# Thirty-eight expert tiles placed inside the routing steps of an attention and expert kernel, b3 folded into centred weights, the table of tiles made in four parts

## The reference, cut to what matters

```python
x = x + conv(ln_c(x))        # q, k, v by 128 x 64 weights; k, v softmaxed over an image
t = to_tokens(x)
logits = einsum('bsd,de->bse', ln_t(t), Wg)
top_logits, top_idx = top_k(logits, 2);  top_w = softmax(top_logits)
h = einsum('bsd,edf->bsef', ln_t(t), W1)
g = einsum('bsd,edf->bsef', ln_t(t), W3) + b3
t = t + einsum('bse,bsef,efd->bsd', C, silu(h) * g, W2)     # C: top_w at the two chosen experts
```

## Time and profile before

| what | value |
|---|---|
| runs, median (lowest to highest) | 329.83 us (326.42 to 330.59) |
| profiled execution, span | 344.2 us |
| mean granted TensorE clock | 0.787 |
| TensorE busy | 255.7 us, 74% |
| VectorE busy | 233.2 us, 68% |
| ScalarE busy | 184.4 us, 54% |
| GpSimd busy | 182.1 us, 53% |
| moved by DMA | 29.78 MB |

### The profile page before, as it was taken

One profiled execution on the slowest core, in us unless ns is written; L12 is line 12 of the kernel. 1 busy time (PEld: TensorE's weight loads), 2 busy tenths in 40 slices (PEclk: granted clock), 3 DMA queues, 4 the chain that ended last, 5 costly groups with the idle time before them and its releaser, 6 DMA issues.

```text
span 344.2 us, 7292 instructions
## 1 busy us (share of the span) xinstructions
PE 255.7 (74%) x1560; PEld 220.5 (64%) x1561; DVE 233.2 (68%) x835; ACT 184.4 (54%) x471; POOL 182.1 (53%) x233
## 2 busy tenths in 40 slices
PE   4786949474848574340999999999999999999300
PEld 1444636453636463110999999999999899999200
DVE  3658676675655565640688878887888788878823
ACT  2636638273635332310577777776777677777200
POOL 4094274452717273770066656665666557666800
PEclk9986855565555555585799999999999999999855
DMA  4879210110101010131133222221222212136068
GB/s 112 286 229 352 77 55 23 39 35 29 47 16 43 22 54 23 55 101 32 41 85 82 71 59 59 72 62 47 61 61 61 61 54 70 46 93 214 33 203 292
DMA packets 31904, 29.78 MB, mean 87 GB/s; under 512 B 5202, under 2 KB 29588, under 8 KB 31748
## 3 DMA queue, kind: packets, MB, share of 16 engines
q1 hardware_dynamic: 24208, 18.11, 18.2%
q0 software_dynamic: 4320, 8.92, 7.7%
q10 hardware_dynamic: 3348, 2.44, 2.1%
HBM read 17.45 MB, written 12.01 MB: 86 GB/s over the span
## 4 chain that ended last, share of the span: by engine, by line
PE 44%; DVE 19%; issue 14%; POOL 9%; DMA 5%; SPq 3%; ACT 2%; another core or an unknown queue 1%; POOLq 0%; DVEq 0%; ACTq 0%
PE bank L718 6%; PE bank L720 6%; PE bank L719 6%; PE bank L736 6%; PE bank L726 6%; PE bank L740 5%; POOL result_rows L1353 4%; DMA w_all<-result_rows 3%; PE bank L706 2%; DVE stats L994 2%; PE bank L654 2%; POOL w_all L1348 2%; POOL sorted_rows L1311 2%; DVE mean_var L999 2%; SPq L422 1%
## 5 line engine op out<-in xcount | busy, mean ns | idle before, releaser
L1311 POOL DMA_INDIRECT sorted_rows<-row_buf,position x64 | 62.8, 981 | 62.7 <-ACT row_buf L843 44.9
L1353 POOL DMA_INDIRECT result_rows<-w_all,xs x71 | 71.1, 1002 | 21.0 <-issue 19.7
L1348 POOL TENSOR_TENSOR w_all<-y_parts 128x128 f32<-128x128 f32 x71 | 32.7, 460 | 47.5 <-ACT y_parts L930 45.2
L718 PE MATMUL bank<-w_up,xs_hi 128*128 x142 | 54.5, 384 | 0.0
L1234 DVE TENSOR_TENSOR w_all<-bank,b_all 128x384 f32<-128x384 f32 x71 | 39.6, 557 | 21.0 <-PE bank L720 20.6
L925 ACT ACTIVATE act_hi<-bank 128x384 fp32r<-128x384 f32 x71 | 34.9, 492 | 27.9 <-issue 16.9
L720 PE MATMUL bank<-w_up,xs_hi 128*128 x142 | 48.2, 340 | 0.0
L719 PE MATMUL bank<-w_up,xs_lo 128*128 x142 | 48.2, 339 | 0.0
L1254 DVE TENSOR_TENSOR act_lo<-bank,act_hi 128x384 fp32r<-128x384 f32 x71 | 39.1, 551 | 6.4 <-issue 4.4
L736 PE MATMUL bank<-w_down,act_hi 128*128 x213 | 42.9, 309 | 0.8 <-ACT y_parts L930 0.8
L1242 DVE TENSOR_TENSOR act_rows<-w_all 128x384 f32<-128x384 f32 x71 | 39.7, 559 | 2.5
(11 more groups left out here) (166 smaller groups left out, 436.1 us busy)
## 6 DMA issues: line engine op xcount, KB each, us to landing
xs<-sorted_rows SPq DMA_DIRECT2D x71, 65.0 KB
w_all<-result_rows SPq DMA_DIRECT2D x16, 256.0 KB, 4.3
x_all<-x_dram SPq DMA_DIRECT2D x8, 256.0 KB, 3.3
out_dram<-w_all ACTq DMA_DIRECT2D x8, 256.0 KB, 4.1
w_all<-L_ffn_W_dram SPq DMA_DIRECT2D x2, 960.0 KB, 7.9
b_all<-L_ffn_b_dram SPq DMA_DIRECT2D x1, 1536.0 KB, 10.5
w_all<-L_ffn_W_dram SPq DMA_DIRECT2D x2, 576.0 KB, 4.8
result_rows<-w_all,xs POOLq DMA_INDIRECT x71, 2.3
```

The costliest lines, as they stand in the source:

```text
L718: nc.tensor.matmul(o, xs_hi[s.par][:], w[0], start=True, stop=False)
L1311: nc.gpsimd.indirect_dma_start(out=sorted_rows.ap(), out_offset=bass.IndirectOffsetOnAxis(ap=position[u.par][:, c:c + 1], axis=0), in_=row ...
L1348: nc.gpsimd.tensor_tensor(ys[s.ring % RESULTS][:], y_parts[s.par][:, 0, :], y_parts[s.par][:, 1, :], ALU.add).then_inc(y_sum, 1)
L1353: nc.gpsimd.indirect_dma_start(out=result_rows.ap(), out_offset=bass.IndirectOffsetOnAxis(ap=xs[s.ring][:].bitcast(I32)[:, DEST:DEST + 1], ...
```

## The change

* Tiles 0 to 37 run inside routing steps 4 to 8, eight "turns" a step, from turn 2 of step 4; tiles 38 to 70 (`FINAL` = 38) follow behind. All turns are written out, no loop is left.
* A turn of TensorE: transpose the activation of tile s-2, the down product of s-3, the W1 product of s, the transpose of tile s+1, the W3 product of s. Inside the steps fewer banks of PSUM are free, so the down product is "narrow": six products of 128 columns into one 128-column result in place of three of 256. ScalarE then writes the weighed result itself and POOL only scatters it. Behind the steps the form is wide, as before.
* The table is made in four parts (`PHASES`): after unit 2 for tiles 0 to 15, after unit 4 for 16 to 31, after unit 6 for 32 to 47, after unit 7 for 48 to 70. The first three take full tiles only; which numbers of tiles are sure to be full follows from the number of rows.
* SyncE writes all eight paddings behind the load of tile 40 (`PADS_BEHIND`), and loads tile 41 after them.
* b3: channel 127 of a normalised row is replaced by 1. TensorE takes the last row of W1 and W3 away from the others (the row sums to zero, so the products stay) and puts b3 into the last row of W3. The addition of b3 (L1234) goes.
* Keys and values are projected one step earlier; both `keep_busy(8)` and the 24 multiplications go. ScalarE loads the table of silu and the table of exp once per step in steps 4 to 8 (nine loads in all).
* A unit's eight scatters stand in pairs in turns 3 to 6, behind the scatter of a tile's result each.

In a step TensorE's pieces stand thus: turn 0, `transpose_probs`, `rank`, `logits_of_x`, turn 1, `weigh_tokens`, turn 2, `mix_channels`, turns 3 and 4, `spread_br`, `attend`, `count_rows`, turn 5, `transpose_xn` and one `centre_weights`, turns 6 and 7, `project_kv` and a second `centre_weights`. ScalarE has `normalise_t` between turns 2 and 3 and `normalise_x` between 3 and 4. VectorE has `weigh_and_place` between turns 2 and 3, the two halves of a table part (`share_rows`, `fill_slots`) ahead of turns 6 and 7 in steps 3, 5, 7 and 8, and the splitting of centred weights (`split_up`, `split_down`) at the end of steps -1 to 3. An expert's weights are centred in steps -1 (one), 0, 1, 2 (two each) and 3 (one).

The diff, cut to its core; first the constants and SyncE's loads, then TensorE, ScalarE and VectorE:

```diff
+    TURNS = 8
+    FIRST_STEP, FIRST_TURN = 4, 2
+    FINAL = (NU - FIRST_STEP + 1) * TURNS - FIRST_TURN
+    PHASES = ((2, 0, 16), (4, 16, 32), (6, 32, 48), (7, 48, NS))
+    PADS_BEHIND = 40
...
+            for n in range(NS):
+                load_rows(Slot(n, RING, NS))
+                if n == PADS_BEHIND:
+                    sp.wait_ge(count_ready, 1)
+                    for e in range(E):
+                        pad_region(sp, e)
...
+            def centre_weights(e):
+                pe.wait_ge(early_in if e < LOADED_FIRST else late_in, EXPERT_LOADS)
+                at_least(pe, up_lo_ready, e - 1)
+                o = bank_pair[e % 2]
+                nc.tensor.matmul(o[:, 0, 0:F], centre[:], w_all[:, e, 0, :], start=True, stop=True)
+                nc.tensor.matmul(o[:, 1, 0:F], centre[:], w_all[:, e, 1, :], start=True, stop=False)
+                pe.wait_ge(b3_in, 16)
+                nc.tensor.matmul(o[:, 1, 0:F], last_one[:], b3_row[:, e * F:(e + 1) * F],
+                                 start=False, stop=True).then_inc(centred_ps, 1)
...
+            def transpose_rows(s):
+                if s.n == 0:
+                    pe.wait_ge(up_lo_ready, E)
+                    pe.wait_ge(down_lo_ready, E)
+                at_least(pe, xs_lo_ready, s.n)
+                at_least(pe, y_sb, min(s.n - 3, FINAL))
+                pe.wait_ge(xs_in[s.ring], 16 * s.round + 16)
...
+                    o = bank[4][:, P:P + C]
+                    for k in range(KF):
+                        for half in range(2):
+                            nc.tensor.matmul(o, act_hi[s.par][:, k * P:(k + 1) * P], w[k][:, half * C:(half + 1) * C],
+                                             start=(k == 0 and half == 0), stop=False)
...
+            def turn(s):
+                if s is None:
+                    return
+                if s.has(-2):
+                    transpose_act(s.shift(-2))
+                if s.has(-3):
+                    down(s.shift(-3), experts[s.n - 3])
+                if s.has(0) and s.n % TURNS == 0:
+                    load_experts(s)
+                if s.has(1) and (s.n < 0 or wide(s)):
+                    transpose_rows(s.shift(1))
+                if s.has(0):
+                    up(s, 0, experts[s.n])
+                    if s.has(1) and not wide(s):
+                        transpose_rows(s.shift(1))
+                    up(s, 1, experts[s.n])
...
+                if i.n > FIRST_STEP:
+                    nc.scalar.preload_act_table_set("natural_log_exp_and_others")
                 if has_norms(later):
                     rough_rstd(later)
+                if exists(new):
+                    exp_kv(new)
                 if exists(old):
                     exp_gap(old)
+                if i.n >= FIRST_STEP:
+                    nc.scalar.preload_act_table_set("silu_and_others")
+                turn(slot_of_turn(i, 1))
...
-                nc.vector.tensor_tensor(gate[s.par][:], bank[3 + s.par][:, 0:F],
-                                        b3_all[:, ds(e, 1), :].rearrange("p a f -> p (a f)"),
-                                        ALU.add).then_inc(gate_ready, 1)
```

More of the change, by code:

```diff
@@ L393, in run_units, with slot_of_turn, wide, old_slots_with @@
         def run_units(iteration):
-            for i in range(-3, NU + 2):
+            for i in range(-3, NU + 1):
                 iteration(Step(0, i))
[L398 to L419, removed]
+        def slot_of_turn(i, k):
+            n = (i.n - FIRST_STEP) * TURNS + k - FIRST_TURN
+            return Slot(n, RING, NS) if n >= -1 else None
+        def wide(s):
+            return s.n >= FINAL
+        def old_slots_with(s, regular, spare):
+            if s.n < FINAL:
+                return s.n, regular
+            if (s.n - FINAL) % 2 == 0:
+                return (s.n if s.n == FINAL else s.n - 1), regular
+            return s.n - 1, spare
+        def experts_of_step(i):
+            return {-1: (0,), 0: (1, 2), 1: (3, 4), 2: (5, 6), 3: (7,)}.get(i.n, ())
+        def wait_scattered(eng, u):
+            if u.n >= 0:
+                eng.wait_ge(scattered[u.par], 16 * SCATTERS * (u.half + 1))
         def pad_region(eng, e):
@@ L501, in _, with load_rows @@
[L501 to L507, removed]
+            def load_rows(s):
+                for p, (unit, first, _) in enumerate(PHASES):
+                    if s.n == first:
+                        if p == len(PHASES) - 1:
+                            sp.wait_ge(pads_in, 16 * (E + SPARE))
+                        sp.wait_ge(table_ready, p + 1)
+                        wait_scattered(sp, Step(0, unit - 1))
+                        wait_scattered(sp, Step(0, unit))
+                at_least(sp, y_out[s.ring], s.round * 16)
+                row = sp.value_load(slot_row[0:1, s.n:s.n + 1], min_val=0, max_val=E * REGION + (SPARE - 1) * P)
+                sp.dma_start(xs[s.ring][:], sorted_rows[ds(row, P), :]).then_inc(xs_in[s.ring], 16)
@@ L517, in load_half @@
             def load_half(k):
[L518 to L522, removed]
+                for u in range(NU):
+                    load_results(Slot(u, LAST_RING, NU), k)
             sp.wait_ge(half_table, 1)
@@ L744, in _, with load_experts @@
             experts = {}
-            def head(s):
-                if s.has(1):
+            def load_experts(s):
+                ahead = min(TURNS, NS - s.n)
+                pe.wait_ge(table_ready, 1 + sum(first <= s.n for _, first, _ in PHASES[1:]))
+                _, values = nc.values_load_multi_w_load_instructions(
+                    slot_expert[0:1, s.n:s.n + ahead], engines=(mybir.EngineType.PE,), min_val=0, max_val=E - 1,
+                    skip_runtime_bounds_check_because="VectorE clamps slot_expert to 0 .. E-1 when it writes it")
+                for i in list(experts):
+                    if i < s.n - 3:
+                        del experts[i]
+                for i, value in enumerate(values):
+                    experts[s.n + i] = value
@@ L762, in _ @@
+            pe.wait_ge(dve_consts, 2)
+            keep_busy(10)
+            pe.wait_ge(pool_consts, POOL_CONSTS)
+            pe.wait_ge(kv_in, 16 * 4)
+            run_units(iteration)
+            for n in range(FINAL, NS + 3):
+                turn(Slot(n, RING, NS))
         @block.scalar
@@ new lines, in turn @@
+            def turn(s):
+                if s is None:
+                    return
+                if s.has(-2):
+                    copy_act_t(s.shift(-2))
+                if s.has(-3):
+                    scale_result(s.shift(-3))
+                if s.has(1) and (s.n < 0 or wide(s)):
+                    copy_rows_t(s.shift(1))
+                if s.has(0):
+                    silu(s)
+                if s.has(1) and not (s.n < 0 or wide(s)):
+                    copy_rows_t(s.shift(1))
@@ L1151, in iteration @@
             def iteration(i):
                 later, new, old = i.shift(2), i.shift(1), i.shift(-1)
-                if has_norms(later):
+                weights = experts_of_step(i)
+                phase = [p for p, (unit, _, _) in enumerate(PHASES) if old.n == unit]
+                turn(slot_of_turn(i, 0))
+                if i.n < 0 and has_norms(later):
+                    find_shift(later)
+                if exists(new):
+                    max_kv(new)
+                if i.n >= 0 and has_norms(later):
```

737 lines of the change are left out of this document (377 added, 360 removed).

## The result

The changed kernel takes 361.69 us (360.53 to 363.54, 4 runs), the kernel before beside it 328.47 (326.42 to 330.59). The ratio is 1.103, 95% interval 1.0973 to 1.1087. The forecast was 320, its range 302 to 348.

A forecast was written before the change was run, and what follows sets the result against it. TensorE bounds the tiles, with room under late routing and the hole. 159.2 (steps 4 to 8) + 71 + 3 = 233.2 replaces 247.1; with +2 +2, -9.9: 344.2 becomes 334.3, less 14.4: 320 us, range 302 to 348.

The forecast's parts named there:

- I sum against 344.2 and take 14.4 off: Whole kernel: changes summed against the profiled 344.2 us, then its 14.4 us excess over the median 329.83 subtracted.
- some 4 us: Hole between routing and tiles: part of the 14.4 may lie there, taking up to this from the gain.
- Early steps: I take +2: Routing before the tiles: centring products mostly fill TensorE's idle time, POOL's splitting goes; +2 us, bounds -5 and +15.
- a tile costs TensorE 2.57: Tiles in steps 4 to 8: 2.15 us plus 0.42 for three more weight loads; 38 tiles cost 97.7.
- Clock: I add 4: Steps 4 to 8: 4 us for short spells of TensorE at half clock after recurring waits.
- half-clock rival: Steps 4 to 8: waits drop TensorE to half clock; slower, above 336.4 us, 355 with a third so; chance 0.21.
- ScalarE at the head: 10: Head of a step: TensorE waits some 2.5 us behind ScalarE's table loads and root, in four steps: 10 us.
- The table in parts: 10: Steps 5, 7 and 8: VectorE's table parts hold TensorE 3.4 us each: 10 us, bounds 0 and 14.
- The first tile: 10: Step 4: TensorE waits for the first tile's scatter and load, some 8 us, and 2 until the first product.
- 33 tiles: 71, paddings 3: Behind the steps: 33 wide tiles at 2.15 take 71 us; TensorE waits 3 us for SyncE's eight paddings.
- End +2: Behind the last tile: 21.6 us stays, plus 2 us because POOL works one turn later.

The follow-up runs named there:

- the second profile: The kernel before, unchanged, profiled once more: 331.18 us, span 329.4; unit 3's choice to the last product took 233.1 us.

## Why the prediction was wrong

The miss is 41.7 us. Summed against the profile shown, before the 14.4 came off, the forecast was a span of 334.3; it came to 360.5. Those 26.2 are 15.0 early (unit 3 chosen at 92.5, forecast 77.5), 13.0 from there to the last product (338.7 - 92.5 = 246.2, forecast 233.2) and -1.8 at the end (21.8, forecast 23.6). With the 14.4, and 1.2 between span and median, it is 41.8. In steps 4 to 8 TensorE was busy 152.9 us where I had summed 127.2 (97.7 + 25.5 + 4), and idle 19.2 where I had summed 32: the work was dearer and the waits shorter than I took, so the 13.0 are a difference of two larger errors.

* *"I sum against 344.2 and take 14.4 off"*: failed. The sum replaced the stretch that held the excess, with pieces that did not hold it, so it was taken off twice. The allowance of "some 4 us" was too small: 14.0 of the excess lay in this stretch. Set against the 233.1 of the second profile, the forecast stretch of 233.2 would have been no gain at all.
* *"Early steps: I take +2"*: failed; it was 17, above the upper bound of 15. I put the centring products into TensorE's idle time and counted POOL's missing splitting as a gain, but did not ask what POOL's remaining rounding was queued behind. Two chains hold 10.5 of the 17, and each hides the other: taking one away gave little, both 10.3. For splitting two experts in a step and for the first part of the table I had no term here; they go with the rest.
* *"a tile costs TensorE 2.57"*: mis-sized, 3.13, above even the upper bound of 2.15 + 0.84. The six products cost 0.32 to 0.37, as I took (0.42); the rest I had no term for. 38 x 0.56 is 21 us, an estimate at full clock.
* *"Clock: I add 4"*: mis-sized, at least 9.9. The half-clock rival was the right mechanism: its mark, a mean clock below 0.87 over the steps, came (0.85), with steps of 36.9 and 37.1 us. By its own price it gives 336 at a clock of 0.87 and some 340 at 0.85; alone it does not explain 361.7. The Trainium skill, "TensorE: Matmul & The Clock Gate", section "HAM oscillation", describes work broken by waits that starts slow each time. The trace agrees: 0.50 for 6.8 us behind the 2.64 us gap.
* *"ScalarE at the head: 10"*: right in place and in sum. The four gaps are 2.62, 2.64, 3.52 and 1.00, together 9.8; single ones lie up to 1.5 off the 2.5 that I took. The next activation starts at 160.58, 0.01 after the load ends; so the drain of about 1.38 us that the Trainium skill gives ("ScalarE: Activation LUTs", section "What ACT_TABLE_LOAD costs") does not show here either.
* *"The table in parts: 10"*: too high. TensorE's gaps beside the parts in steps 5 and 7 are 0.88, 0.70, 0.97 and 1.55, 4.1 in all. Without tiles a part costs some 3 us of a step. *"The first tile: 10"*: too high as well; TensorE idles 3.81 ahead of it.
* *"33 tiles: 71, paddings 3"*: 74.1, right in sum by luck. The eight paddings took SyncE 7.4 us (255.3 to 262.7), below the 9 that I took as least, and no gap stands at tile 41. The 3 us are in the tiles: at the mean of the kernel before (159.1 / 71 = 2.24) 33 of them take 73.9. *"End +2"*: nothing.

## What to carry to other kernels

Before work is moved into the gaps of a stage, profile that stage twice and sum against the shorter one; time that only one execution shows is no room to fill. When a piece is moved to another engine or place, list what it is queued behind there and who waits for it in order: each of two chains of about equal length hides the gain of removing the other. A wait put into a dense stage costs its own length and then the slow clock behind it, here about as much again.

## What the hardware showed unexpectedly

* The same kernel on the same kind of chip gave routing steps of 17.2 us in one execution and 14.1 in another, with TensorE's 11.30 us unchanged. VectorE's instructions are as long in both (the four of the statistics 0.87 us); its waits between them differ: 1.29 against 0.18 us ahead of L999, 1.7 against 0.1 ahead of L1008. What it waited for is open.
* W2 products of 128 columns follow each other at 0.13 us, those of 256 columns at 0.16 or less: half the columns make a product only about a sixth cheaper.
* 48 small multiplications of ones per step, adding work to the busiest engine, made the kernel 9.9 us faster by holding the clock.
* In the profile without centring the granted clock reads 1.00 from the choice of unit 2 to that of unit 3 (69.6 to 90.6 us), yet the product with 512 columns that starts at 85.05 takes 2.07 us, as at 0.50 in the earlier trace rows. The length of a known product is a second witness for the clock. In the runs without loads and with ones that product takes 1.02 us in step 5, so there the 1.00 holds.
